# Squares and chunk sums of the last feed-forward layer moved to VectorE, with the gelu table asked for ahead

## The reference, cut to what matters

```python
def _ternary_linear(x, w):
    ...
    rms = jnp.sqrt(jnp.sum(x * x, axis=-1, keepdims=True)) / jnp.sqrt(jnp.asarray(d, x.dtype))
    x_norm = x / (rms + EPS)
    return jnp.einsum('bsd,fd->bsf', x_norm, w_q)
h = jax.nn.gelu(_ternary_linear(x, w_up), approximate=False)     # 512 features for each token
return _ternary_linear(h, w_down)
```

## Time and profile before

| | us |
|---|---|
| median of 3 runs | 891.64 |
| lowest and highest | 887.48, 894.52 |
| the profiled execution, its own time | 889.47 |
| span from first to last instruction in it | 887.7 |
| PE, DVE, ACT, POOL busy | 773.4, 657.8, 480.2, 356.5 |
| mean granted clock of TensorE | 0.96 |

### The profile page before, as it was taken

How to read it: one execution, slowest core, us unless ns; L and a number is a source line. 1 busy time by engine, 2 the same in 40 slices (tenths; PEclk the granted TensorE clock), 3 DMA queues, 4 the chain that set the end, 5 groups by cost and what they waited for, 6 DMA issues and landing times.

```text
span 887.7 us, 18946 instructions
## 1 busy us (share of the span) xinstructions
PE 773.4 (87%) x6109; PEld 421.4 (47%) x6179; DVE 657.8 (74%) x2253; ACT 480.2 (54%) x998; POOL 356.5 (40%) x904
## 2 busy tenths in 40 slices
PE   2777689999999898978899999999999988968876
PEld 1446334343445454546565544555454544544454
DVE  7677757888878877776888888987888867548340
ACT  3433245565647456656656665467655654734732
POOL 8884101121325444445465322244333425353134
PEclk9998889999999989999999999999999998989997
DMA  8598812112304366534746422145324253054000
GB/s 297 138 198 197 141 35 37 31 40 44 81 4 112 81 146 133 102 72 82 162 108 120 101 52 56 38 98 100 82 59 89 57 114 79 12 110 80 2 1 12
DMA packets 123810, 77.70 MB, mean 88 GB/s; under 512 B 8184, under 2 KB 122048, under 8 KB 123584
## 3 DMA queue, kind: packets, MB, share of 16 engines
q1 hardware_dynamic: 123712, 76.50, 39.7%
HBM read 41.90 MB, written 32.90 MB: 84 GB/s over the span
## 4 chain that ended last, share of the span: by engine, by line
PE 60%; DVE 16%; issue 7%; POOL 5%; ACT 5%; DMA 4%; SPq 2%; another core or an unknown queue 1%; DVEq 0%; POOLq 0%; ACTq 0%
PE ob L1310 10%; PE mb L1258 8%; PE eb L1286 5%; PE eb L1287 4%; PE side L1178 3%; PE side L1169 3%; PE side L1186 2%; DVE junk L1781 2%; PE eb L1281 2%; PE eb L1290 2%; ACT probs L1504 2%; DMA QW<-bounce 2%; DVE mx L1789 2%; PE side L1105 2%; PE side L1113 2%
## 5 line engine op out<-in xcount | busy, mean ns | idle before, releaser
L1504 ACT ACTIVATE probs<-eb 128x512 f32<-128x512 f32 (+1 forms) x512 | 274.4, 568 | 194.9 <-PE eb L1287 94.1
L1781 DVE CUSTOM_DVE_ANT_0 junk<-mb,maskq_add 128x512 bf16<-128x512 f32 x256 | 169.5, 688 | 46.4 <-PE mb L1258 25.5
L1310 PE MATMUL ob<-probs,V 128*32 128x256 f32 (+1 forms) x2048 | 130.6, 372 | 2.4 <-ACT probs L1504 2.1
L1076 POOL TENSOR_SCALAR nm<-mx 128x8 bf16<-128x8 f32 x80 | 19.9, 249 | 238.5 <-DVE mx L1781 135.2
L1286 PE MATMUL eb<-maskk_add,identb 128*128 128x512 bf16 x256 | 98.0, 383 | 10.0 <-issue 7.4
L1789 DVE TENSOR_REDUCE mx<-mb 128x1 f32<-128x512 f32 x128 | 83.5, 685 | 25.8 <-PE mb L1258 24.4
L1258 PE MATMUL mb<-KS,QP 128*128 128x512 bf16 x222 | 81.2, 392 | 13.7 <-DVE mx L1781 6.8
L1287 PE MATMUL eb<-QP,KS 128*128 128x512 bf16 x239 | 91.1, 381 | 0.0
L980 POOL TENSOR_SCALAR rstd<-mv 128x2 f32<-128x2 f32 x64 | 16.6, 260 | 175.3 <-DVE mv L1567 174.1
L1310 PEld LDWEIGHTS ob<-probs,V 128*32 128x32 f32 x2048 | 54.7, 109 | 59.6 <-issue 30.1
L1381 ACT ACTIVATE hn<-X,nshift,rstd 128x128 f32<-128x128 f32 x80 | 35.1, 486 | 47.5 <-POOL nshift L987 47.3
(11 more groups left out here) (200 smaller groups left out, 1597.9 us busy)
## 6 DMA issues: line engine op xcount, KB each, us to landing
QP<-bounce SPq DMA_DIRECT2D x48, 256.0 KB, 5.6
KS<-bounce SPq DMA_DIRECT2D x32, 384.0 KB, 6.8
bounce<-scratch SPq DMA_DIRECT2D x48, 192.0 KB, 2.2
bounce<-scratch SPq DMA_DIRECT2D x64, 128.0 KB, 2.1
KS<-bounce SPq DMA_DIRECT2D x32, 192.0 KB, 4.2
bounce<-scratch SPq DMA_DIRECT2D x16, 384.0 KB, 3.0
bounce<-scratch SPq DMA_DIRECT2D x16, 256.0 KB, 3.0
bounce<-scratch SPq DMA_DIRECT2D x48, 64.0 KB, 1.8
```

The costliest lines, as they stand in the source:

```text
L1310: ins = nc.tensor.matmul(bank[32 * j:32 * j + 32, S - n:S], v_of(core, kt, 4 * g + j), pr[:, (j % 2) * n:(j % 2 + 1) * n], start=(first_ a ...
L1504: nc.scalar.activation(probs[:, u % PROBS, 0:n], eb[:, u % 2, 0:n], ACT.Exp, scale=SCALE[core.p]).then_inc(probs_by[1], 1)
L1781: ins = V_.tensor_tensor_reduce(junk[:, e.n % 2, :], bank, maskq_add[:, t, :], 1.0, NEG_EXP, ALU.add, ALU.max, mx[slot][:, t, h:h + 1])
```

## The change

The step `square` goes from ACT to DVE and takes in the two additions of `fold`; the step `fold` on POOL is dropped; `squares` on PE waits for one event instead of two. Where the planned list of ACT has `gelu` of a run directly behind its `up 0 kept`, ACT also applies the gelu to a spare tile of 128x2 between them. The planner's costs are set to the new steps, and its ranks are changed, so that the order of all engines is written anew.

```diff
-             ("pe", "up 1", 1.06, ("up 0 kept",)), ("act", "gelu", 2.5, ("up 1",)), ("act", "square", 2.4, ("gelu",)),
-             ("pe", "down", 1.96, ("gelu",)), ("pool", "fold", 2.8, ("square",)), ("pe", "squares", 0.6, ("fold",)), ("dve", "square sums", 0.2, ("squares", "down")),
+             ("pe", "up 1", 1.06, ("up 0 kept",)), ("act", "gelu", 2.5, ("up 1",)), ("dve", "square", 2.1, ("gelu",)),
+             ("pe", "down", 1.96, ("gelu",)), ("pe", "squares", 0.6, ("square",)), ("dve", "square sums", 0.2, ("squares", "down")),
...
-URGENT = {("end", 2): 1, ("end", 4): 2, ("to0", 3): 3, ("to1", 1): 3, ("to1", 6): 1, ("to1", 7): -1, ("to3", 5): 3}
-LATER = {("end", 2): 2, ("end", 4): 3, ("end", 5): 3, ("to0", 3): 2, ("to0", 6): -2, ("to0", 7): 2, ("to1", 1): 2, ("to1", 5): 1, ("to1", 7): -3}
-AFTER = {(2, 0): -1, (2, 4): 2, (2, 7): -2, (3, 2): 3, (3, 7): 1}
-RANK = {"turn": -1, "nm": 0, "row": -1, "chain": 0.8, "keep": 0.5, "chain on TensorE": 2.8, "max": 3.0, "exp": 3, "av": 4}
+URGENT = {("end", 2): 1, ("end", 4): 2, ("to0", 3): 3, ("to1", 1): 3, ("to1", 7): -1, ("to2", 5): -1, ("to3", 5): 3}
+LATER = {("end", 2): 2, ("end", 4): 3, ("end", 5): 3, ("to0", 3): 2, ("to0", 5): 2, ("to0", 6): -2, ("to0", 7): 2, ("to1", 1): 2, ("to1", 3): 3,
+    ("to1", 5): 1, ("to1", 7): -3}
+AFTER = {(2, 0): 2, (2, 4): 2, (2, 5): 2, (2, 7): -2, (3, 0): -1, (3, 2): 3, (3, 7): 1}
+RANK = {"turn": -1, "nm": 0, "row": -1, "chain": 0, "keep": 0.5, "chain on TensorE": 2.8, "max": 3.0, "exp": 3, "av": 4}
...
+_acts = [e for _, e in ORDER["act"]]
+GELU_NEXT = {a.run for a, b in zip(_acts, _acts[1:]) if a.kind == "up 0 kept" and b.kind == "gelu" and a.run is b.run}
...
-                    yield "fold"
-                    pool.wait_ge(sq_ready[l], 2 * N_END(run) + 1)
-                    sq = f32_scratch[l]
-                    link(G.tensor_tensor(sq[:, 0:2 * S], sq[:, 0:2 * S], sq[:, 2 * S:4 * S], ALU.add))
-                    G.tensor_tensor(sq[:, 0:S], sq[:, 0:S], sq[:, S:2 * S], ALU.add).then_inc(sq_ready[l], 1)
...
-                    pe.wait_ge(sq_ready[l], 2 * N_END(run) + 2)
+                    pe.wait_ge(sq_ready[l], N_END(run) + 1)
...
+                    if run in GELU_NEXT:
+                        nc.scalar.activation(warm[:], constant[:, 0, :], ACT.Gelu)
                     yield "gelu"
...
-                    yield "square"
-                    act.wait_ge(ffn_kept[l], n * 4 + 4)
-                    nc.scalar.activation(f32_scratch[l][:, 0:FC * S], xs[l][:], ACT.Square).then_inc(sq_ready[l], 1)
...
                     stats_of(run, X[b])
+                    yield "square"
+                    dve.wait_ge(ffn_kept[l], n * 4 + 4)
+                    sq = f32_scratch[l]
+                    link(V_.tensor_tensor(sq[:, 0:FC * S], xs[l][:], xs[l][:], ALU.mult))
+                    link(V_.tensor_tensor(sq[:, 0:2 * S], sq[:, 0:2 * S], sq[:, 2 * S:4 * S], ALU.add))
+                    V_.tensor_tensor(sq[:, 0:S], sq[:, 0:S], sq[:, S:2 * S], ALU.add).then_inc(sq_ready[l], 1)
                     yield "square sums"
```

## The result

| | before | after |
|---|---|---|
| median, us | 889.64 (887.46 to 894.52, 6 runs) | 900.76 (897.36 to 905.85, 6 runs) |
| the profiled execution | 889.47 | 897.36 |
| its span | 887.7 | 895.6 |

The change makes the kernel slower: the ratio is 1.0132, interval 1.0097 to 1.0166, that is 11.1 us. The prediction of 887.4 was wrong in sign; of the cases that it weighed, *DVE is late* (903.1) came nearest. The profiled execution of after is the fastest of its six, so the profiles show less of the loss, 7.9 us, than the medians.

The account below looks back on a forecast made before the run. PE (87% busy) was taken to bound the kernel, then the last `end` chains after 845 us. ACT -1, end -0.35, DVE +2.2, lanes -2, ranks -2 gave -3.15 us: 887.4 us, own range 883 to 893, 8-in-10 range 874 to 903.

Parts of the forecast that it names:

- DVE is late: Rival, maxima between 390 and 805 us: each of six squares costs PE its full 2.3 us, 903.1 us; chance 0.16.
- DVE beside attention: Maxima behind a square on DVE: one mean wait of 0.36 us for each of six, 2.2 us lost; bounds 0 and 13.9.
- PE under 94% from 500 to 700 us: Sign in the full stretch: PE's busy share falling under 94% there would show DVE late and the prediction wrong.
- -1 (ACT): Squares removed from ACT between exponentials in six of eight chains: 1 us gained; bounds -6.3 and 0.
- -2 (lanes): `end` chains beside the attention free their lanes earlier, which helps where PE lacks work: 2 us gained; bounds 17 and 0.
- -2 (ranks): New ranks, chain steps ahead of ACT's `keep` copies and other entries moved: 2 us gained; bounds 11.8 either way.
- the 1.95 of the end: Last chain: no filler between `down` and `squares`, so `squares` comes at about 880.3 for 882.25, 1.95 us gained.
- The end: Last two chains, after the attention: 1.95 us gained less 1.6 lost at POOL's root, 0.35 us gained as a whole.
- The collision of DVE's square with POOL's root: Last but one chain: DVE's square beside POOL's `root 3` of the last chain, 1.6 us lost; bounds 0 and 2.3.
- The gelu's table: Table load behind `up 0 kept`: the spare gelu does not bring it earlier; priced at nothing, bounded by 0.6 us.
- Mutual blocking of DVE and POOL: Rival, all along: six squares lose 0.93 us and hold a POOL chain 1.2, half reaching PE, 893.8 us; chance 0.06.
- PE's direct waits for maxima: Sign at PE's waits on maxima, 8.7 us in 24 waits before: up by about 2 us.

Follow-up runs that it names:

- e6: e4 with each square on DVE cut to one product on 256 columns, 0.42 us for 2.33; 888.64 us, ratio 0.9986.
- e4: Order of before kept, each square put on DVE at its gelu's place, ACT's square and POOL's fold taken out, spare gelu kept; 902.56 us, ratio 1.0165.
- e5: The kernel after with its new order, each square on DVE cut to one product on 256 columns; 891.29 us, ratio 1.0030.
- e8: The kernel before with only the last chain's square on DVE, its fold and the nine fillers ahead of its `squares` gone; 886.58 us, ratio 0.9972.
- e3: The kernel after without the spare gelu; 903.72 us, ratio 1.0163.
- e9: e4 with the square's first product on DVE made three times, 4.8 us for each square; 919.67 us, ratio 1.0331.
- e1: The kernel after with the four rank tables of before; 904.71 us, ratio 1.0193.

## Why the prediction was wrong, point by point

**The first step that failed is "DVE beside attention".** It charged each of six squares one mean wait of 0.36 us, 2.2 in all. In the order of before the six cost 8.3 us at the squares themselves, 1.4 each, and the attention as a whole grew by 12.3 (e6 to e4). The place that the rival *DVE is late* named was right; its price of 2.3 was nearly reached at two of the six (2.4 and 2.1). The reason against it was the error. "From 500 to 800 us alone DVE has 66 us left" counts idle time wherever it lies. Of the 142 us that DVE idles between 110 and 845 us in before, 119 end at something that PE made: most of the time DVE waits for the engine that it feeds. What counts is how long before PE's need a maximum is done, and that was 0.33 us at the second square. Nor was "PE reached 96 to 97% beside a DVE at 83 to 87%" evidence: only one of the six squares lies between 500 and 700 us, and even there e4 pays 1.6. For the same reason the sign that I named for this rival, PE under 94% from 500 to 700 us, did not appear, and it was the wrong sign.

**In the changed kernel itself**, whose order was planned with the squares on DVE, the six cost only 3.2 us at the squares (e5 to after), 0.5 each. From e5 to after all eight squares' 15.3 us of DVE cost 9.5 by the medians. In the profiles 4.5 of them lie beside the attention (730.5 to 735.0 us) and 4.0 in the end (38.6 to 42.6), 1.9 of these being TensorE's clock, whose cause is open (last section). The forecast had 2.2 and 1.6 for the two places.

**The second step that failed are the gains beside the attention: -1 (ACT), -2 (lanes), -2 (ranks).** With these and the 1.95 of the end, e5, where four fifths of DVE's new time are out, should lie some 7 us under before. Its ratio is 1.0030 (0.9995 to 1.0064), that is 2.7 us above, at best 0.4 under. In its profile the end is 5.9 shorter than before and the attention 7.7 longer: the new order moves time from one to the other. What in it makes the attention longer stays open. So of the 14 us between the forecast of -3 and the measured 11, some 5 are DVE's time (9 for 3.8) and some 9 are gains that e5 does not show. The ranks were no term of their own at all: +19 us on the old steps, -4 on the new ones, so to price them apart from the steps, as "-2", was a mistake of form. In the old order the gains of ACT and of the lanes can't be told from nothing: e6 has ACT and POOL relieved, with 3.4 us of DVE left in, and is 1.2 us under before, unresolved. The 1 us for ACT's square does show there in the twins, all of it at the first square (1.0 less than in before).

**The end.** The gain of 1.95 for fillers and fold is right (e8 alone: 0.9972, and `squares` right behind `down`). The collision of DVE's square with POOL's root was 1.3 us, for 1.6 predicted. The end as a whole gained 1.9 where I had 0.35. e5, with the collision almost gone, gains 5.9, of which 1.6 are TensorE's clock: the last chain's two `up` products take 1.84 and 2.07 us in before and 1.13 each in e5 (last section). **The gelu's table** was right: the load does not come earlier, and without the spare gelu nothing changes for the better (e3).

**Mutual blocking of DVE and POOL** was seen at single squares, not all along: in e4 one of the eight products of 1024 columns was held up (2.10 us, last section), in after none (1.19 to 1.22). PE's direct waits for maxima grew as foreseen, by about 2 us on the line of the earlier trace rows:

```profile
PE mb L1256 <- DVE mx L1792: 10.7, 15, 2.4
```

It was 8.7 us in 24 waits of at most 1.4. But this sign does not speak for the squares. All waits of PE that end at a maximum, from 110 to 860 us, are 16.3 us in before and 20.8 in after, and 20.8 in e5 too, so here it is the new order that made them. In the old order they do grow with the square: 15.9, 21.1 and 28.5 us in e6, e4 and e9.

## What to carry to other kernels

Before work is moved to an engine that feeds the bounding one, measure the cover at the place: the time from the end of the feeding instruction to the moment its user wants it. Spare time elsewhere in the list does not help; at the place followed here all beyond the cover was paid in full, and where the granted clock fell behind the wait (e9), more than that. A cheap test is a dose: make the moved piece tiny and then three times as long in the same order, and read the slope before any order is tuned again; set twins side by side to see at which places it is paid. Move only the piece whose new engine is idle there (here the last chain alone), and do not price tuned ranks apart from the steps that they were tuned for.

## What the runs showed of the hardware

The square with its two additions, each on two SBUF inputs, takes 2.33 us on DVE, but beside POOL's wide instructions nearly twice that. In e4, at the third square:

```profile
486.86 2.10 DVE L1763 TENSOR_TENSOR scratch<-xs 128x1024 f32<-128x1024 f32 x1
...
487.94 1.49 POOL L1001 CAST scratch<-xs 128x512 bf16<-128x512 f32 x1
...
488.99 0.98 DVE L1764 TENSOR_TENSOR scratch<-scratch 128x512 f32<-128x512 f32 x1
489.51 1.48 POOL L1003 TENSOR_TENSOR scratch<-xs,scratch 128x512 bf16<-128x512 f32 x1
490.01 1.26 DVE L1765 TENSOR_TENSOR scratch<-scratch 128x256 f32<-128x256 f32 x1
```

2.10 + 0.98 + 1.26 = 4.3 us, and a PE wait of 2.1 behind it. The negation of maxima is hit as well: in after it took 1.15 us at worst, where 0.24 is its median:

```profile
L1074 POOL TENSOR_SCALAR nm<-mx x80: 236/244/1152, 98.8 to 837.6; 128x8 bf16<-128x8 f32 x80
```

The Trainium skill (SBUF — State Buffer, "Who interferes with whom") says that the later of two such instructions waits for the whole of the other one. The trace of after agrees: in the end of after POOL's 1.10 us end at 875.32, just past the end of DVE's at 875.24.

The end of e5 is 4.0 us shorter than that of after, for 3.8 us less of DVE. The root and the last `squares` account for about 1.6 of it; 1.9 are TensorE's clock. The windows over the last chain's two `up` products, in after and then in e5:

```profile
881.00:887.00 6.00, 5.29 (x14) 3.01 (x14) 0.61 (x2) 1.60 (x5) 0.20 (x1) 0.55 0.07 22
```

```profile
878.00:882.00 4.00, 3.16 (x13) 1.98 (x15) 0.61 (x2) 1.66 (x5) 0.17 (x1) 1.00 0.11 33
```

The granted clock is 0.55, near the lower of the two levels, against 1.00; each `up` product takes 2.07 us there against 1.13, 1.9 us together. In after PE had stood idle 2.27 us ahead of that chain, waiting for the root that the square had held up, and in e5 1.74. But the length of that wait does not decide it. e1 and then e8, the turn of the rows ahead of the products and the first of the two:

```profile
889.13 0.44 PE L1092 MATMUL side<-ident,hn 128*128 128x128 f32 x2 [2.73 <-ACT hn L1378]
890.03 1.13 PE L1175 MATMUL side<-hT,W 128*128 128x256 f32 x4 [0.46 <-ACT hT L1371]
```

```profile
867.90 0.44 PE L1105 MATMUL side<-ident,hn 128*128 128x128 f32 x2 [1.67 <-ACT hn L1391]
868.80 2.07 PE L1188 MATMUL side<-hT,W 128*128 128x256 f32 x4 [0.46 <-ACT hT L1384]
```

e1 waited 2.73 us and its granted clock behind that is 1.00 (890 to 893 us); e8 waited 1.67, as before did, and has 0.54 (868 to 874 us). So it is not shown that the square brought the clock down in after; the cause of these 1.9 us stays open.
